# Attention block and routed expert layer on one core: v, gate, k and q products in rounded parts, in another order, and half of w2 fetched late

## The reference, cut to what matters

```python
x = layernorm(x)
q = silu(x @ wq); k = sigmoid(x @ wk); v = x @ wv
f = 1 - k                       # decay of the state, per channel and token
# recurrent state over tokens, with a sign that follows f > 0.5:
#   S = S * f + k v ;  o = q S
gate = sigmoid(x @ wg1 @ wg2)   # 256 x 128, then 128 x 256
out = layernorm(o * gate) * norm_w @ wo
y = x + out
e = argmax(layernorm(y) @ centroids.T)
out = y + sigmoid(best) * (xs + relu(layernorm_e(xs) @ w1[e].T + b1[e]) @ w2[e].T + b2[e]) + (1 - sigmoid(best)) * xs
```

## Time and profile before

| | us |
|---|---|
| three timed runs | 680.75, 682.22, 683.26 (median 682.22) |
| the profiled execution | 684.39 |
| its span, first to last instruction | 682.6 |
| TensorE, VectorE, ScalarE, GpSimd busy in it | 597.5, 345.1, 280.0, 225.9 |
| mean granted TensorE clock | 0.944 |

### The profile page before, as it was taken

One profiled execution on the slowest core, in us unless ns is written; L12 is line 12 of the kernel. 1 busy time (PEld: TensorE's weight loads), 2 busy tenths in 40 slices (PEclk: granted clock), 3 DMA queues, 4 the chain that ended last, 5 costly groups with the idle time before them and its releaser, 6 DMA issues.

```text
span 682.6 us, 12519 instructions
## 1 busy us (share of the span) xinstructions
PE 597.5 (88%) x3638; PEld 503.7 (74%) x3639; DVE 345.1 (51%) x864; ACT 280.0 (41%) x671; POOL 225.9 (33%) x384
## 2 busy tenths in 40 slices
PE   3979998999999899977632499999999999999992
PEld 2547675776868677766521499999999999999992
DVE  2395968859595969677237032233233232332331
ACT  3554766476676667451430122222222222222220
POOL 6614261434434261611012113323323323333321
PEclk9999999999999999979665699999999999999997
DMA  9900015140312302020222855545545546545300
GB/s 318 401 9 1 0 32 94 31 91 15 72 42 70 56 32 63 32 62 32 63 63 72 309 197 209 206 178 190 220 169 209 210 169 218 204 171 222 132 28 2
DMA packets 26844, 83.48 MB, mean 122 GB/s; under 512 B 3437, under 2 KB 13039, under 8 KB 20656
## 3 DMA queue, kind: packets, MB, share of 16 engines
q1 hardware_dynamic: 21120, 67.98, 31.1%
q0 software_dynamic: 4992, 14.45, 5.6%
q10 hardware_dynamic: 688, 0.52, 0.2%
HBM read 70.33 MB, written 13.52 MB: 123 GB/s over the span
## 4 chain that ended last, share of the span: by engine, by line
PE 65%; DVE 10%; DMA 6%; issue 4%; ACT 2%; POOL 1%; DVEq 0%; SPq 0%; POOLq 0%
PE bank_a L1129 21%; PE bank_c L1143 20%; DMA arena<-x 4%; PE bank_l L885 4%; PE bank_c L999 3%; PE bank_a L897 3%; PE bank_a L926 3%; DVE arena L1194 2%; DVE arena L1205 2%; PE bank_a L935 2%; PE bank_b L977 1%; PE bank_b L963 1%; PE bank_b L1117 1%; DMA arena<-routed_rows,take_now 1%; PE bank_a L942 1%
## 5 line engine op out<-in xcount | busy, mean ns | idle before, releaser
L1459 DVE TENSOR_TENSOR arena<-bank_a,b_col 128x512 f32<-128x512 f32 x78 | 54.0, 692 | 193.6 <-PE bank_a L1129 179.8
L1129 PEld LDWEIGHTS bank_a<-masks,arena 128*128 128x128 f32 x1248 | 146.9, 194 | 1.9
L1129 PE MATMUL bank_a<-masks,arena 128*128 128x128 f32 x1248 | 147.0, 277 | 0.0
L1143 PE MATMUL bank_c<-w_sb,arena 128*128 x624 | 141.5, 380 | 1.6 <-ACT arena L860 0.9
L1143 PEld LDWEIGHTS bank_c<-w_sb,arena 128*128 128x128 f32 x624 | 115.5, 190 | 16.8 <-issue 2.7
L885 PEld LDWEIGHTS bank_l<-arena,k_mix 128*128 128x128 f32 x448 | 65.8, 198 | 50.8 <-ACT k_mix L681 37.6
L1194 DVE TENSOR_TENSOR arena<-arena 128x256 f32<-128x256 f32 x224 | 90.4, 445 | 9.6 <-PE bank_l L885 9.4
L860 ACT ACTIVATE arena<-arena 128x512 f32<-128x512 f32 x78 | 45.0, 622 | 107.7 <-PE bank_c L1143 103.3
L885 PE MATMUL bank_l<-arena,k_mix 128*128 128x128 f32 x448 | 73.8, 290 | 16.7 <-DVE arena L1205 14.8
L850 ACT ACTIVATE masks<-bank_b,b_col,g_col 128x128 f32<-128x128 f32 x78 | 31.4, 453 | 132.9 <-PE bank_b L1117 132.9
L897 PE MATMUL bank_a<-arena 128*128 128x512 f32 x160 | 83.5, 621 | 0.0
(11 more groups left out here) (137 smaller groups left out, 751.6 us busy)
## 6 DMA issues: line engine op xcount, KB each, us to landing
arena<-w SPq DMA_DIRECT2D x39, 1024.0 KB
routed_rows<-arena SPq DMA_DIRECT2D x8, 1026.0 KB, 8.7
arena<-x SPq DMA_DIRECT2D x16, 512.0 KB, 6.5
w_sb<-w SPq DMA_DIRECT2D x8, 1024.0 KB, 14.7
arena<-b SPq DMA_DIRECT2D x1, 1024.0 KB, 4.6
arena<-routed_rows,take_now POOLq DMA_INDIRECT x39
out<-k_mix,put_now POOLq DMA_INDIRECT x39, 2.5
arena<-wk SPq DMA_DIRECT2D x1, 256.0 KB, 3.9
```

What stands on the lines that cost most here:

```text
L1129: m = pe.matmul(bank_a[k // 4][:, k % 4 * P:(k % 4 + 1) * P], w1_now[t.par][:, i * F + k * P:i * F + (k + 1) * P], xl_t[t.par % 2][:, i * ...
L1143: m = pe.matmul(bank_c[p][:, 0:D], h_act[:, k * P:(k + 1) * P], w2_sb[:, bass.ds(e * (FC * D) + k * D, D)], start=(k == 0), stop=(k == FC ...
L1459: dve.tensor_tensor(h_sb[:, n * 512:(n + 1) * 512].rearrange("p (k t) -> p k t", t=P), bank_a[n][:, :].rearrange("p (k t) -> p k t", t=P), ...
```

## The change

It has five parts.

1. **Rounded parts.** k, q, v and gate products are made in float32r, which holds a rounded f32. Each operand is split: high is the value rounded, low is the rest rounded. A product becomes three: high x high, low x high and high x low, all into the same bank. Of the normalized x ScalarE writes high while it copies it from PSUM, and VectorE makes low with a subtraction (`xn_low_part`). The weights are split once at the start. The output product stays plain f32.
2. **Gate in one product.** wg1 @ wg2 is made once at the start (`gate_weights`), stands beside wv, and `v_gate` makes v and gate together with 512 columns, one chunk of tokens at a time in one bank: 8 groups of three products. g1 is gone.
3. **Order.** The v/gate groups stand between the levels. k and q stand behind the levels, q's two heads around the key-value products. The diagonals come last. ScalarE evicts v and gate between the levels in pieces of 128 x 256, and k, decay and q behind them. VectorE has the x statistics, decays and q multiplications behind the levels, the residual before them. GpSimd makes q times decay and q k first and the tree of decays after.
4. **Start.** ScalarE waits for wg1, wv and wg2 before it normalizes the first x.
5. **Late w2.** w2 now lies in `arena`. Its first half overlaps the x, xn, qk and k/q weight buffers, so only experts 4 to 7 are fetched at the start and experts 0 to 3 after the last sequence's diagonals, in front of the residual load of that round on SP's queue.

```diff
-        w2_sb = sb("w2_sb", [P, E * FC * D], F32)
-        PHASE1_AB = 24576
-        ARENA = 33808
-        arena_at = nc.sbuf_base
+        W2_ALL = E * FC * D
+        W2_LATE = W2_ALL // 2
+        PHASE1_AB = W2_ALL + 19712
+        ARENA = PHASE1_AB + 9232
+        arena_at = -(-nc.sbuf_base // 32) * 32
         arena = sb("arena", [P, ARENA], F32)
+        assert nc.sbuf_base == arena_at + 4 * ARENA
...
+        w2_sb = arena[:, 0:W2_ALL]
+        lay = Layout(0, W2_LATE)
         x_sb = [lay.take(TJ * D) for _ in range(2)]
         xn = lay.take(TJ * D)
-        xn_t = lay.take(DC * T)
+        xn_high = lay.take_rounded("xn_high", DC * T)
+        xn_low = lay.take_rounded("xn_low", DC * T)
+        qk = lay.take(H * T)
...
+            def fetch_w2(experts):
+                for e in experts:
+                    w = slice(e * FC * D, (e + 1) * FC * D)
+                    sp.dma_start(w2_sb[:, w], w2_t[:, w]).then_inc(s_w2, 16)
+            fetch_w2(range(E // 2, E))
 
             def step(a, b, c, nxt):
+                if a is None and b is not None:
+                    need(sp, s_dz, H, b, H)
+                    fetch_w2(range(E // 2))
...
+                if c is not None:
+                    need(pool, s_zn, TJ, c, 0)
+                    need(pool, s_base, TJ, c, 0)
+                    need(pool, s_aff, 1, c, 0)
+                    double_norm(c)
                 if nxt is not None:
                     need(pool, s_xn, TJ, nxt, 0)
                     norm("x", nxt)
+                if a is None and b is not None:
+                    need(pool, s_on, TJ, b, 0)
+                    norm("o", b)
                 if a is not None:
                     dec = decay[a.par]
                     need(pool, s_f0, H, a, H)
+                    need(pool, s_q, H, a, H)
+                    need(pool, s_o, 2, before(a, 2), 2)
+                    pool.tensor_tensor(queries(kq[a.par]), q_raw.rearrange("p (m s) -> p m s", s=2 * P),
+                                       tree(dec, 0).rearrange("p (m s) -> p m s", s=2 * P), ALU.mult).then_inc(s_q0, 1)
+                    need(pool, s_k, H, a, H)
+                    need(pool, s_dz, H, a, 0)
+                    pool.tensor_tensor(split_chunks(qk), split_chunks(q_raw), keys(kq[a.par]), ALU.mult).then_inc(s_qk, 1)
...
+                for l, h in ((1, 1), (2, 0), (2, 1)):
+                    of(b, mix, l, h)
+                def evict(j):
+                    of(a, v_copy, j)
+                    of(a, gate_sigmoid, j)
+                evict(0)
...
+            act.wait_ge(s_wvg, 48)
+            copy(vg_half(wvg_high, 0), wv_sb).then_inc(s_vghigh, 1)
             x_norm(Step(0, 0, 2))
+            act.wait_ge(s_w1t, 1)
+            copy(wg1_t, bank_b[1][:, 0:DC * P]).then_inc(s_w1tc, 1)
+            act.wait_ge(s_w12, 1)
+            copy(vg_half(wvg_high, 1), bank_b[0][:, :].rearrange("p (c n) -> p c n", c=DC)).then_inc(s_vghigh, 1)
...
+            def channels(high, low, h, bank, i):
+                x = slice(i * T, (i + 1) * T)
+                w = slice(i * D + h * P, i * D + (h + 1) * P)
+                pe.matmul(bank[:, :], high[:, w], xn_high[:, x], start=(i == 0), stop=False)
+                pe.matmul(bank[:, :], low[:, w], xn_high[:, x], start=False, stop=False)
+                return pe.matmul(bank[:, :], high[:, w], xn_low[:, x], start=False, stop=(i == DC - 1))
...
+            def gate_weights():
+                pe.wait_ge(s_wvg, 48)
+                for i in range(DC):
+                    m = pe.transpose(bank_b[1][:, i * P:(i + 1) * P], wg1_sb[:, i * P:(i + 1) * P], ident[:, :])
+                m.then_inc(s_w1t, 1)
+                pe.wait_ge(s_w1tc, 1)
+                for i in range(DC):
+                    m = pe.matmul(bank_b[0][:, i * D:(i + 1) * D], wg1_t[:, i * P:(i + 1) * P], wg2_sb, start=True, stop=True)
+                m.then_inc(s_w12, 1)
+            def v_gate(a, j, i):
+                if j < 2:
+                    need(pe, s_xnt, DC, a, DC)
+                    need(pe, s_xlo, DC, a, DC)
+                else:
+                    need(pe, s_v, TJ, a, j - 1)
+                    need(pe, s_gate, TJ, a, j - 1)
+                x = slice(i * T + j * P, i * T + (j + 1) * P)
+                w = slice(i * 2 * D, (i + 1) * 2 * D)
+                pe.matmul(bank_a[j % 2][:, :], xn_high[:, x], wvg_high[:, w], start=(i == 0), stop=False)
+                pe.matmul(bank_a[j % 2][:, :], xn_high[:, x], wvg_low[:, w], start=False, stop=False)
+                m = pe.matmul(bank_a[j % 2][:, :], xn_low[:, x], wvg_high[:, w], start=False, stop=(i == DC - 1))
...
+                for l, h, i in ((1, 0, 0), (1, 1, 0), (2, 0, 1), (2, 1, 1)):
+                    of(b, level, l, h)
+                    of(a, v_gate, i, h)
...
+                for l, h, half, j in ((5, 0, 0, 0), (5, 1, 0, 1), (6, 0, 1, 0), (6, 1, 1, 1)):
+                    of(b, level, l, h)
+                    of(c, out_proj, half, j)
+                if b is None and a is not None:
+                    pe.wait_ge(s_whigh, 2)
+                    pe.wait_ge(s_wlow, 2)
+                for h in range(H):
+                    for i in range(DC):
+                        of(a, k_proj, h, i)
                 of(b, k_transposes)
-                of(a, g1_proj, 1)
+                for i in range(DC):
+                    of(a, q_proj, 0, i)
                 of(b, key_values)
-                of(a, v_proj, 0)
-                of(a, v_proj, 1)
-                of(a, gate_proj, 0)
+                for i in range(DC):
+                    of(a, q_proj, 1, i)
...
-                of(a, gate_proj, 1)
-                of(a, diagonal, 0)
                 if b is not None:
                     outputs(b, 0, None if c is None else lambda n: affinity(c, n))
+                of(b, outputs, 1)
+                of(a, diagonal, 0)
                 of(a, diagonal, 1)
-                of(b, outputs, 1)
 
             pe.wait_ge(s_const, 1)
-            pe.wait_ge(s_wqk, 32)
+            gate_weights()
...
+            def xn_low_part(a, i):
+                need(dve, s_xnt, DC, a, i + 1)
+                x = slice(i * T, (i + 1) * T)
+                dve.tensor_tensor(xn_low[:, x], bank_a[i][:, :], xn_high[:, x], ALU.subtract).then_inc(s_xlo, 1)
...
+                of(nxt, x_stats)
+                of(a, decays, 0)
+                of(a, decays, 1)
+                of(a, q_mult, 0)
                 of(b, states)
+                of(a, q_mult, 1)
                 if b is not None and c is None:
                     centre()
-                output(b, c, a)
+                of(b, first_half)
+                of(c, affinities)
+                of(b, gating, 1)
+                of(a, attn_diagonal, 0)
+                of(a, attn_diagonal, 1)
```

262 lines of the change are left out of this document (105 added, 157 removed).

## The result

| | before | after |
|---|---|---|
| median of the runs | 681.49 us | 696.36 us |
| the profiled execution | 684.39 | 692.41 |
| ratio, with its 95% interval | | 1.022 (1.019 to 1.025) |

The change made the kernel slower. The median is 6 us above the 690 that were forecast and inside the range of 671 to 712. The profiled execution of after is the quickest of its four (692.41 to 698.21); its granted clock was 0.945, the others' 0.936 to 0.940. The profiled execution of before, in turn, is slower than its timed ones. Two executions, one of experiment 1's kernel (1088.72 us) and one of the kernel before (819.70), ran at a much lower granted clock and count in no figure here.

A forecast was written before the change was run, and what follows sets the result against it. TensorE's work was taken to bound each attention step, with 1.1 us of waits. 684.4 + 9 (start) + 2 (clock) - 4 (seven steps) = 691.4; timed runs had been 2.2 lower, so 690 us, range 671 to 712.

The forecast's parts named there:

- TensorE's floor: TensorE's work in an attention step: 13.8 us removed, 48 rounded products at 0.215 added, so 35.9 falls to 32.4 us.
- rival B: Rounded products in the attention steps cost a full record, 0.43 us each: 748 us; at 0.30, 700. Chance 0.10.
- The six waits: Waits the moved code makes in each attention step: 4.5 us together, so a step is 36.9 us.
- ScalarE's evictions: In a step, v and gate evictions and o's normalization ahead of key mixing of levels 3 and 4: 0.8 us wait.
- Affinities behind the copies of x1: In a step's tail, outputs follow x1's transposes at once and affinities need both copies: 1.0 us wait.
- Diagonals behind q k: At a step's end, diagonals wait for qk, which GpSimd makes after the query product: 0.4 us.
- Seven steps: Second to ninth step start in the attention part: 258 us instead of 262, 4 less.
- The start: First round: everything waits for the gate weights, next levels start near 40.5, 9 us later, plus 2 for the clock.
- Late w2 and the end: Late w2 loads land well before the first down product, last rounds and expert part unchanged: cost 0.
- A: Faster: TensorE stays the bound in the steps, waits lie beside its work; steps 33.5, kernel 666 us. Chance 0.15.
- C: Thinner steps let the clock fall once in each, 1.7 us a step, 12 in seven: 702 us. Chance 0.14.
- D: No change: the start costs 5 instead of 11, or steps are a microsecond shorter: 680 to 685. Chance 0.13.

The follow-up runs named there:

- experiment 1: The changed kernel's order with plain f32 products, one for each three and no subtractions: 702.12 us, ratio 1.029 against the kernel before.
- experiment 10: Changed kernel with experiment 5's first round, q k ahead of the query product, first v/gate product waiting only for its half of x: 677.00 us, ratio 0.995.
- experiment 4: The kernel before with only half of w2 fetched late, behind the last diagonal: 681.67 us, ratio 1.000.
- experiment 5: Changed kernel, first round reordered: wk and wq split first, k, gate weights, q, then v and gate: 683.54 us, ratio 1.004 against before.
- experiment 6: Changed kernel with 27 plain products ahead of the first round's diagonals, filling TensorE's pause: 695.85 us, ratio 1.022 against before.
- experiment 2: Changed kernel with only high x high of each three products: 697.85 us, ratio 1.026 against before.
- experiment 3: Changed kernel without the high x low products, two of three kept: 693.06 us, ratio 1.017 against before.
- experiment 8: Change in the old order with experiment 5's first round; x statistics later, second q multiplication ahead of the residual, k/q groups one place later: 675.26 us, ratio 0.992.
- experiment 9: The kernel before, plain f32, with x statistics behind x1's moments and the second q multiplication ahead of the residual: 677.97 us, ratio 0.996.
- experiment 11: experiment 8 with seven plain products, results unread, ahead of level 2 in steady rounds: 673.51 us, ratio 0.990 against before.
- experiment 12: experiment 11 with GpSimd's tree of decays ahead of the next x's norm in round one, 14 filler products in round two: 670.60 us, ratio 0.986.

## Why the prediction was right, step by step

The direction was right, and so was its cause, the loss in the first round. How near the number came is in part luck: a step's two terms were off in opposite directions, and the gain of the seven steps came from elsewhere than forecast.

**TensorE's floor.** The mis-sized term is the rounded product. It was put at 0.215 and is 0.229: the first round's 24 for k and q run from 27.91 to 33.22 without a break, 0.30 for the first and 22 x 0.228 behind it. So 48 take 11.0 us instead of 10.3.

```profile
27.91 0.47 PE L936 MATMUL bank_a<-xn_high,wk_high 128*128 128x512 f32 x1 [2.64 <-ACT wq_high L707]
28.21 0.39 PE L937 MATMUL bank_a<-xn_high,wk_low 128*128 128x512 f32 x1
...
33.22 0.39 PE L938 MATMUL bank_a<-xn_low,wq_high 128*128 128x512 f32 x1
```

Besides, the first of a group behind plain products is followed after 0.30 to 0.32 (194.31, 194.61) and once 0.41 instead of 0.23, eleven times a step: 1.0 in all. The working 35.9 - 13.8 + 11.0 + 1.0 gives 34.1, and 34.09 were measured where 32.4 were forecast. The price is near the value chosen, and far from both ends, 0.10 and 0.86; rival B falls with it. TensorE's share of a step, 88% in the forecast, was 91%.

**The six waits.** Forecast 4.5, measured 3.2. The transposes behind the diagonal: 0.49 for 0.5. The first v/gate product behind the low parts: 0.95 for 1.3. Level 1 and what follows it behind subtractions and statistics: 0.83 and 0.33, at levels 2 and 3, where 0.5 stood. ScalarE's evictions: no wait at levels 3 and 4 where 0.8 stood. Affinities behind the copies of x1: absent where 1.0 stood, since the outputs themselves wait 0.37 for VectorE's states and the copies are done by then; in experiment 1, where TensorE is later, 0.57 appears there. Diagonals behind q k: under 0.1 where 0.4 stood, and experiment 10 got nothing large from it. A wait of 0.21 for the keys of level 1 was not forecast. So a step of 32.4 + 4.5 = 36.9 was in truth 34.1 + 3.2 = 37.3: two errors of 1.7 and 1.3 with opposite signs, which is luck.

**Seven steps.** Forecast 4 less than before, measured 4.7 less, but not for the reason given. Of it 2.0 is the second step, as forecast, and 3.3 is before's step of 40.54 against 37.28: a load of x that came late and a fall of the clock behind it, both absent in experiment 4's trace. The other five are together 0.6 longer than before's. The forecast compared its 36.9 with before's mean of 37.4, which held that step. Against a before without it, as in experiment 4, the steady steps gained nothing.

**The start.** Forecast 9 for the order and 2 for the clock, measured 12.3. The terms behind 17.1 sum to 22.3, so the forecast's own working gives 39.4 and not 40.5, 7.6 later instead of 9. Measured, the first v/gate product was at 18.40: the two products of the gate weights took 2.08 and the transposes 1.91 where 1.0 and 0.9 stood. The 24 products and their evictions took 6.7 for 6.1; a loading of ScalarE's table (1.28) between the evictions was not counted, and TensorE waited 0.88 there. The diagonals came at 39.83 and took 3.80 for 1.9. Experiments 5 and 10 show that it was the first round's order: in another, the second step begins at 36.2 and 33.4. The clock had 1.8 of it by the diagonals' length; experiment 6, which was to show it in the time, does not.

**Late w2 and the end.** Both 0 forecast; experiment 4 is 1.000, the rest of the trace +0.5.

**The rivals.** A, TensorE as the bound, is refuted: experiments 2 and 3 take work away and get a seventh of it or nothing in most steps. In the last step with a new sequence the share is larger, 2.2 of 6.3 us and 1.6 of 3.3, and still far from all. C, the clock, did not come about in the steps of after's profiled execution, but it stood close by: experiments 2, 3, 8 and 10, which have less work on TensorE or shorter steps, met it in half or more of the later steps, and experiments 1 and 5, which have not, in two and in one. Experiment 6 has after's steady rounds, and its trace takes 264.3 us for the seven steps, 7.0 more than after's, with four falls in them. So C's mechanism does reach this kernel in some executions; how much of it is in after's slower ones is not shown. D is refuted by the start's 12.3. The median lies 6 above the forecast; the profiled execution is 1 above the 691.4 of the sum.

## What to carry to other kernels

- Before pricing cheaper products, ask what a step would be without them. Where it is a chain over three engines, it gives back a small part of what one engine loses; the edits of the steady rounds that paid here moved VectorE's work out of the levels' chain (experiments 8 and 9).
- Thinner TensorE work can cost the clock, and one trace need not show it: compare the granted clocks of all executions. Filling the longest wait with products that nobody reads can then be worth more than the products saved.
- A difference between two traces can be one long step of one execution. Compare step by step, and with a third trace, before it is put down to the change.
- A new order for the steady rounds need not be the order of the first round, where nothing runs beside it. Here that one round held nearly all of the loss.

## What the runs showed of the hardware

A rounded product of 512 columns follows the last after 0.229 us and has one record; a plain one has two and takes 0.86. Three rounded ones, 0.69, are thus cheaper than one plain.

A fall of the clock for 3.4 us cost a step 1.0 us in experiments 8 and 10 (36.83 against 35.81, and 38.07 against 37.04), 1.4 in experiment 5 (38.67 against 37.28) and 1.6 in experiment 1 (39.57 against 37.96): in none of these more than half its length, 1.7.

GpSimd's power of 128x4 took 2.85 us while VectorE's mask copy ran, and 1.05 otherwise. From experiment 11, GpSimd's timeline:

```profile
23.09 2.85 POOL L588 TENSOR_TENSOR x_rstd<-x_vareps,minus_half 128x4 f32<-128x4 f32 x1
```

and VectorE's:

```profile
23.89 2.02 DVE L1411 CAST masks<-arena 128x3584 uint8<-128x3584 f32 x1
```

In experiment 12 the tree of decays stood there, and took 5.51 instead of 3.48 us. The Trainium skill (SBUF — State Buffer, Who interferes with whom) says that the two engines share one pair of ports as a lock for a whole instruction; both lengths, longer by 1.8 and 2.0 for a copy of 2.0, agree with that. Which of the two waited does not follow from the order of the records: the power's begins 0.80 us ahead of the copy's, and it is the one that got longer.
